# Experts' feed-forward tiles: a two-buffer loop rewritten as straight code with layer 2 a tile behind layer 1

## The reference

```python
hn2 = _layernorm(x, ln2_g, ln2_b).reshape(-1, h)
logits = hn2 @ gate_w + gate_b
idx = jnp.argmax(logits, axis=-1)
mid = jax.nn.relu(jnp.einsum('th,ehf->etf', hn2, w1) + b1[:, None, :])
y = jnp.einsum('etf,efh->eth', mid, w2) + b2[:, None, :]
moe = y[idx, jnp.arange(hn2.shape[0])]
return x + moe.reshape(b, s, h)
```

## Time and profile before

| what | us |
|---|---|
| median of 3 runs | 1405.19 (1399.92 to 1406.61) |
| profiled execution, from first to last instruction (span) | 1443.4 |
| attention stage, to about | 1056 |
| sorting stage, to the first layer 1 | 1094.95 |
| first layer 1 to the last tile's layer 1 | 329.63 |
| last layer 1 to the end of the span | 18.8 |

### The profile page before, as it was taken

How to read it: one execution, slowest core, us unless ns; L and a number is a source line. 1 busy time by engine, 2 the same in 40 slices (tenths; PEclk the granted TensorE clock), 3 DMA queues, 4 the chain that set the end, 5 groups by cost and what they waited for, 6 DMA issues and landing times. The chain is left out here.

```text
span 1443.4 us, 27529 instructions
## 1 busy us (share of the span) xinstructions
PE 1296.1 (90%) x7138; PEld 922.7 (64%) x7138; DVE 942.6 (65%) x6185; ACT 854.2 (59%) x2061; POOL 682.9 (47%) x816
## 2 busy tenths in 40 slices
PE   7868799999999999999999999989828888888886
PEld 6445665666667567576566666655417778877775
DVE  4878979987997996997998899444162222222221
ACT  2335588788697787878878879778611222222221
POOL 3566373553555456346356355320133556655553
PEclk9989999999999999999999999999857999999998
DMA  5210651641842663374274174185132552554451
GB/s 183 86 54 37 155 97 41 166 90 37 180 97 63 129 133 78 85 158 83 73 157 93 35 179 92 42 202 90 44 108 85 179 172 66 195 194 154 154 178 23
DMA packets 104988, 161.15 MB, mean 112 GB/s; under 512 B 35058, under 2 KB 58232, under 8 KB 100760
## 3 DMA queue, kind: packets, MB, share of 16 engines
q1 hardware_dynamic: 86760, 106.51, 31.6%
q0 software_dynamic: 18096, 53.19, 11.6%
HBM read 161.81 MB, written 46.53 MB: 144 GB/s over the span
## 5 line engine op out<-in xcount | busy, mean ns | idle before, releaser
L1013 ACT ACTIVATE pt<-fr 128x512 f32<-128x512 f32 x512 | 277.0, 617 | 25.7 <-PE fr L613 22.5
L1244 DVE CUSTOM_DVE_ANT_0 over<-fr,over 128x256 f32<-128x256 f32 x512 | 198.0, 419 | 85.8 <-ACT over L1023 79.2
L1023 ACT ACTIVATE over<-fr 128x256 f32<-128x256 f32 x512 | 178.7, 391 | 52.9 <-PE fr L613 48.5
L613 PE MATMUL fr<-qs,ks 128*128 128x512 f32 x512 | 189.1, 452 | 3.7 <-DMA qs<-cT 1.3
L613 PE MATMUL fr<-ks,qs 128*128 128x256 f32 x512 | 170.0, 350 | 7.7 <-DVE nmax L1244 3.7
L1358 POOL TENSOR_TENSOR m<-m,e 128x1024 f32<-128x1024 f32 x32 | 75.9, 2370 | 184.9 <-DVE m L1180 184.9
L613 PEld LDWEIGHTS fr<-qs,ks 128*128 128x128 f32 x512 | 87.1, 188 | 86.5 <-issue 50.5
L613 PE MATMUL fr<-kd,qs 128*128 128x256 f32 x512 | 137.0, 282 | 0.0
L814 PE MATMUL ob<-pt,v 128*32 128x512 f32 x1024 | 136.4, 605 | 0.6 <-ACT pt L1013 0.5
L613 PEld LDWEIGHTS fr<-ks,qs 128*128 128x128 f32 x512 | 97.1, 190 | 43.6 <-DVE nmax L1244 25.0
L613 PE MATMUL xs<-VW,pT 128*128 128x256 f32 x512 | 120.0, 389 | 1.8 <-issue 1.7
(11 more groups left out here) (211 smaller groups left out, 2943.7 us busy)
## 6 DMA issues: line engine op xcount, KB each, us to landing
parts_d<-parts SPq DMA_DIRECT2D x32, 512.0 KB, 4.2
ks<-parts_d SPq DMA_DIRECT2D x128, 128.0 KB, 3.9
qs<-parts_d SPq DMA_DIRECT2D x128, 128.0 KB, 4.1
xy_d<-xy SPq DMA_DIRECT2D x32, 256.0 KB, 4.0
kd<-diff_d SPq DMA_DIRECT2D x128, 64.0 KB, 4.0
xyf<-xy_d SPq DMA_DIRECT2D x32, 256.0 KB, 4.2
rows_d<-row SPq DMA_DIRECT2D x32, 256.0 KB, 3.4
diff_d<-diff SPq DMA_DIRECT2D x16, 256.0 KB, 2.3
```

What stands on the lines that cost most here:

```text
L613: return pe.matmul(o, l, r, start=first, stop=last)
L1013: act.activation(pt[:, t % 2, h, :], fr_bank(b, "st", 16 * g + n)[:, :], ACT.Exp, scale=D ** -0.5)\
L1023: act.activation(over[:, (16 * g + n + 64 * b) % NREL, :], fr_bank(b, "fs", 16 * g + n)[:, S // 2:S], ACT.Relu)\
L1244: v.tensor_tensor_reduce(rest, fr_bank(b, "fs", 16 * g + n)[:, 0:S // 2], rest, 1.0, -BIG, ALU.add, ALU.max, nmax[:, g % 2, 4 * h + t:4 * ...
```

## The change

- The loop is gone: all 39 tiles are straight code, and waits compare with constants.
- PE's order becomes: layer 1 of n+1, `turn` of n+2, layer 2 of n. ACT and DVE follow: relu of n+1 comes ahead of the work on tile n's output.
- `rows` and `w1s` have three buffers (`NBUF`), asked for three tiles ahead; `w2s` keeps two and is asked for when layer 2 of n-1 is done, for n+1.
- b2 is repeated for all 128 partitions on the host and joined to the rows of w2 (128 x 2304 floats); the gather of b2 is gone. `resb` of a tile now waits for its w2 rows.
- All gather indices are made once (`wix`, `tix`); the copies to `gix` and `sid` are gone.

```diff
-            def tile(j, q, more, last=False):
-                pe.wait_ge(turned_out[q], reads(j, 1, 1))
-                pe.wait_ge(w1_in[q], reads(j, 16, 16))
...
-                if not last:
-                    turn(j + q, 1 - q)
-                pe.wait_ge(w2_in[q], reads(j, 16, 16))
-                pe.wait_ge(mid_act[q], reads(j, 1, 1))
...
-                    v.tensor_scalar(gix[:, q, :], rec[:, bass.ds(2 * j + q + 2, 1), :].rearrange("p a c -> p (a c)"),
-                                    0.0, None, ALU.add).then_inc(gix_ready[q], 2)
...
+            v.tensor_scalar(wix[:, :, :], wrow[:, :, :], float(P), dc("part"), ALU.mult, ALU.add).then_inc(weights_known, 1)
...
+            v.tensor_scalar(tix[:, :], EO[1][:, 0:ETILES], float(TOK), None, ALU.add).then_inc(tokens_known, 1)
...
+            turn(0)
+            turn(1)
+            first_layer(0)
+            pe.wait_ge(tokens_known, 1)
+            for n in range(ETILES):
+                if n + 1 < ETILES:
+                    first_layer(n + 1)
+                if n + 2 < ETILES:
+                    turn(n + 2)
+                second_layer(n)
...
+            def residual(n):
+                q = n % 2
+                dve.wait_ge(rows_in[n % NBUF], 16 * (n // NBUF + 1))
+                dve.wait_ge(w2_in[q], 16 * (n // 2 + 1))
+                wait(dve, ot_ready[q], n // 2)
+                v.tensor_tensor(resb[:, q, :], rows[:, n % NBUF, DM:2 * DM], w2s[:, q, FT * DM:], ALU.add)\
+                 .then_inc(resb_ready[q], 1)
...
+            middle(0)
+            residual(0)
+            for n in range(ETILES):
+                if n + 1 < ETILES:
+                    middle(n + 1)
+                    residual(n + 1)
+                finish(n)
...
+            fetch_w1(0)
+            fetch_w2(0)
+            fetch_w1(1)
+            fetch_w2(1)
+            fetch_w1(2)
+            pool.wait_ge(tokens_known, 1)
+            for n in range(NBUF):
+                fetch_rows(n)
+            for n in range(ETILES + 1):
+                q = n % 2
+                if n + NBUF < ETILES:
+                    pool.wait_ge(turned[q], n // 2 + 1)
+                    pool.wait_ge(resb_ready[q], n // 2 + 1)
+                    fetch_rows(n + NBUF)
+                    pool.wait_ge(mid_act[q], n // 2 + 1)
+                    pool.wait_ge(mid_dve[q], n // 2 + 1)
+                    fetch_w1(n + NBUF)
+                if 1 <= n < ETILES - 1:
+                    pool.wait_ge(l2_full[1 - q], (n - 1) // 2 + 1)
+                    pool.wait_ge(resb_ready[1 - q], (n - 1) // 2 + 1)
+                    fetch_w2(n + 1)
+                if n > 0:
+                    scatter(n - 1)
```

More of the change, by code:

```diff
@@ L400, in pair @@
             return [sem(f"{name}{n}") for n in range(2)]
-        gix_ready = pair("gix_ready")
-        rows_in, w1_in, w2_in, b2_in = pair("rows_in"), pair("w1_in"), pair("w2_in"), pair("b2_in")
+        weights_known, tokens_known = sem("weights_known"), sem("tokens_known")
+        rows_in, w1_in = [[sem(f"{name}{n}") for n in range(NBUF)] for name in ("rows_in", "w1_in")]
+        w2_in = pair("w2_in")
         turned, turned_out = pair("turned"), pair("turned_out")
@@ L1438, in program @@
         past = sb("past", [P, ETILES, E])
[L1439 to L1445, removed]
+        keep = sb("keep", [P, 2, ETILES])
+        expert = sb("expert", [P, ETILES])
+        wrow = sb("wrow", [P, 2, ETILES])
+        token = sb("token", [P, ETILES])
+        wix = sb("wix", [P, 2, ETILES], U32)
+        tix = sb("tix", [P, ETILES], U32)
+        rows = sb("rows", [P, NBUF, 2 * DM])
         znT2 = sb("znT2", [P, 2, KT, P])
-        w1s = sb("w1s", [P, 2, W1COLS])
-        w2s = sb("w2s", [P, 2, FT, DM])
-        b2s = sb("b2s", [P, 2, DM])
+        w1s = sb("w1s", [P, NBUF, W1COLS])
+        w2s = sb("w2s", [P, 2, W2COLS])
         mid = sb("mid", [P, 2, FT, P])
@@ L1456, in dc @@
             return dcon[:, a:a + n]
[L1458 to L1472, removed]
         block = ctx.enter_context(nc.Block())
@@ L1528, in _ @@
             settle(v.tensor_reduce(ex, past[:, :, :], AX.X, ALU.add))
-            v.memset(keep[:, 0:2], 0.0)
+            v.memset(keep[:, 0, 0:NBUF], 0.0)
+            v.memset(keep[:, 1, 0:2], 0.0)
             settle(v.tensor_scalar(ex, ex, float(E - 1), None, ALU.min))
[L1531 to L1535, removed]
+            v.tensor_tensor(keep[:, 0, NBUF:], expert[:, NBUF:], expert[:, 0:ETILES - NBUF], ALU.is_equal)
+            settle(v.tensor_tensor(keep[:, 1, 2:], expert[:, 2:], expert[:, 0:ETILES - 2], ALU.is_equal))
+            settle(v.scalar_tensor_tensor(wrow[:, :, :], keep[:, :, :], float(E),
+                                          ex.unsqueeze(1).to_broadcast((P, 2, ETILES)), ALU.mult, ALU.add))
+            v.tensor_scalar(wix[:, :, :], wrow[:, :, :], float(P), dc("part"), ALU.mult, ALU.add).then_inc(weights_known, 1)
             settle(v.tensor_tensor(base[:, :], cum[:, c, :], cum[:, 0, :], ALU.subtract))
@@ L1586, in tile, with finish @@
[L1586 to L1590, removed]
-                v.tensor_tensor(ot[:, q, :], EO[q][:, 0:DM], resb[:, q, :], ALU.add).then_inc(ot_ready[q], 1)
-            tiles(dve, tile)
+            def finish(n):
+                q = n % 2
+                dve.wait_ge(l2_full[q], n // 2 + 1)
+                dve.wait_ge(resb_ready[q], n // 2 + 1)
+                wait(dve, scattered[q], 16 * (n // 2))
+                v.tensor_tensor(ot[:, q, :], EO[q][:, 0:DM], resb[:, q, :], ALU.add).then_inc(ot_ready[q], 1)
@@ L1600, in _, with turn, first_layer @@
               .then_inc(count_full, 1)
-            def turn(j, q):
-                pe.wait_ge(rows_in[q], reads(j, 16, 16))
+            def turn(n):
+                q = n % 2
+                pe.wait_ge(rows_in[n % NBUF], 16 * (n // NBUF + 1))
+                wait(pe, turned_out[q], n // 2)
                 for k in range(KT):
-                    ins = pe.transpose(ET[q][:, k * P:(k + 1) * P], rows[:, q, k * P:(k + 1) * P], ident[:, :])
+                    ins = pe.transpose(ET[q][:, k * P:(k + 1) * P], rows[:, n % NBUF, k * P:(k + 1) * P], ident[:, :])
                 ins.then_inc(turned[q], 1)
-            def tile(j, q, more, last=False):
-                pe.wait_ge(turned_out[q], reads(j, 1, 1))
-                pe.wait_ge(w1_in[q], reads(j, 16, 16))
+            def first_layer(n):
+                q = n % 2
+                pe.wait_ge(turned_out[q], n // 2 + 1)
+                pe.wait_ge(w1_in[n % NBUF], 16 * (n // NBUF + 1))
+                wait(pe, mid_act[q], n // 2)
+                wait(pe, mid_dve[q], n // 2)
                 for half in range(2):
@@ L1636, in _, with turned_to @@
             ins.then_inc(tokens_full, 1)
-            turn(0, 0)
-            tiles(pe, lambda j, q, more: tile(j, q, more, isinstance(j, int) and 2 * j + q == ETILES - 1))
+            turn(0)
[8 more added lines that the diff above has]
+                second_layer(n)
         @block.scalar
         def _(act):
-            def turned_to(j, q):
-                act.wait_ge(turned[q], reads(j, 1, 1))
+            def turned_to(n):
+                q = n % 2
+                act.wait_ge(turned[q], n // 2 + 1)
                 for k in range(KT):
@@ L1647, in turned_to, with middle @@
                 ins.then_inc(turned_out[q], 1)
-            def tile(j, q, more):
-                act.wait_ge(l1_full[q], reads(j, 2, 1))
+            def middle(n):
+                q = n % 2
+                act.wait_ge(l1_full[q], 2 * (n // 2) + 1)
+                wait(act, l2_full[q], n // 2)
+                bias = w1s[:, n % NBUF, KT * FF:]
                 for f in range(FT // 2):
-                    ins = act.activation(mid[:, q, f, :], EH[2 * q][:, f * P:(f + 1) * P], ACT.Relu,
-                                         bias=w1s[:, q, KT * FF + f:KT * FF + f + 1])
+                    ins = act.activation(mid[:, q, f, :], EH[2 * q][:, f * P:(f + 1) * P], ACT.Relu, bias=bias[:, f:f + 1])
                 ins.then_inc(mid_act[q], 1)
[L1656 to L1660, removed]
+            turned_to(0)
+            turned_to(1)
+            middle(0)
+            for n in range(ETILES):
+                if n + 1 < ETILES:
+                    middle(n + 1)
+                if n + 2 < ETILES:
+                    turned_to(n + 2)
         @block.gpsimd
@@ L1683, in _, with fetch_rows @@
[L1683 to L1704, removed]
+            def fetch_rows(n):
+                gather(rows[:, n % NBUF, :], rows_d, tix[:, n:n + 1], rows_in[n % NBUF], TOK)
@@ L1705, in tile, with fetch_w1, fetch_w2, scatter @@
+            def fetch_w1(n):
+                gather(w1s[:, n % NBUF, :], w1b, wix[:, 0, n:n + 1], w1_in[n % NBUF], E * P - 1)
+            def fetch_w2(n):
+                gather(w2s[:, n % 2, :], w2b, wix[:, 1, n:n + 1], w2_in[n % 2], E * P - 1)
+            def scatter(n):
+                q = n % 2
+                pool.wait_ge(ot_ready[q], n // 2 + 1)
```

(10 more changed lines are left out.)

42 lines of the change are left out of this document (19 added, 23 removed).

## The result

The changed kernel takes 1464.75 us (median of 4 runs, 1460.54 to 1468.91) against 1405.87 for the kernel before beside it: a ratio of 1.0436 [1.041, 1.0463], 4.4% slower, where 1396 was forecast.

A forecast was written before the change was run, and what follows sets the result against it. PE was taken to bound the kernel, with late-message waits in the experts' stage mostly the profiler's. Stall -11, start +1, changes of expert +1 to 2: about -9 from the 1405 median, 1396 us; range 1355 to 1412.

The forecast's parts named there:

- The late messages: Experts' stage: PE's messages of finished work reach DVE and ACT up to 2.5 us late, mostly in the profiled execution.
- The first case: Experts' stage: waits mostly the profiler's, timed runs lose little; 1388 to 1408, centre 1396, chance 0.50.
- The left-over stall: Experts' stage: part of the 54 us excess still present in timed runs, 6 to 16 us, taken as 11.
- Order of PE: Layer 2 of n after layer 1 of n+1: saves 54 us in the profile, 6 to 16 in timed runs.
- straight code: Experts' tiles without the loop: instruction fetches cost 0 to 1 us in all; bound 1 us for each of some 20.
- Joined b2: b2 in w2's rows: 0.13 MB less in each tile, as much more in each load of w2; worth 0.
- index copies: DVE's 0.16 and 0.15 us a tile removed: worth 0, and 0.07 at the very end.
- The hole: Layer 2 of a tile: PE idle between 1220.4 and 1222.48, waiting for DVE's late relu; predicted to go.
- Start: First tiles: later first weights and rows, and `turn` of tile 1 ahead of layer 1, lose 0.3 to 1.5, taken as 1.
- POOL: POOL's gathers: 0.75 us spare a tile becomes about 2; changed waits are met within a plain tile, cost 0.
- The rival that ended slower: Changes of expert: w2 lands 2.3 us late in 14 loads, +32 us, 1428; range 1410 to 1430, chance 0.12.
- Third buffer: Rows asked for three tiles ahead: worth 0 to 4.6 us; extra w1 loads, 3.8 us of DMA, hidden beside PE.

The follow-up runs named there:

- the second profile: The kernel before, unchanged, profiled once more: 1405.71 us, span 1403.9 us.
- run 7: Changed kernel with w2's gather ahead of rows and w1, but PE, ACT and DVE in the order of the kernel before: 1399.95 us.
- run 8: The kernel before with its hardware loop over tiles written out as straight code: 1403.9 us, ratio 1.0001.
- b2_apart: Changed kernel with b2 gathered by itself again just ahead of w2, `resb` waiting for b2 instead of w2: 1460.2 us.
- no_reload: Changed kernel with all weight gathers after each buffer's first fill out of bounds, so they move nothing: 1393.33 us.
- Runs 1 and 5: Changed kernel with w2's gather ahead of rows and w1: 1393.74 us; changed kernel with four row buffers, rows waiting for `resb` of n-1: 1393.56 us.
- run 9: Changed kernel with a third w2 buffer, w2 asked for n+2 where n+1 was, POOL's order kept: 1388.5 us.
- w2_first: Changed kernel with the gather of w2 for n+1 ahead of the gathers of rows and w1 for n+3: 1393.74 us.
- run 10: Changed kernel with w2's gather ahead of rows and w1, and two w1 buffers instead of three: 1435.17 us.

## Why the prediction was wrong
**The late messages: right.** The first case, that most of the 54 us belong to the one profiled execution, holds: the second profile has no such waits. The left-over stall was given as 6 to 16. It is 285.2 - 275.5, less the 2 of the slow clock, so about 8. The 6 had put some 10 us around the span; they are 1.8 (1405.71 and 1403.9).

**Order of PE, straight code: right. Joined b2, index copies: not shown by themselves.** The hole is gone, and the order is worth 5 to 6 us (run 7), the low end of what was given. Unrolling is worth 0 (run 8); the bound of 1 us a fetch came from no row. `b2_apart` is about as slow as the changed kernel, but both have the circle, so it doesn't price the joining. The copies weren't tried alone.

**Start: taken as 1, is about 0.** From the last matmul of the sorting to the first layer 1 it is 6.6 us in both kernels.

**POOL: the step that failed.** It reads: "The waits ahead of POOL's gathers change: rows of n+3 wait for `resb` of n, and behind them stand w1, w2 and the scatter. In a plain tile all of these are met within the tile: 0." For a plain tile this is so: 6.1 to 6.8 us around, under 7.25. But the sum then had only 1 to 2 us for all changes of expert, and weights are loaded 34 times after the first tiles (20 of w1, 14 of w2, the 37.55 MB by which this queue differs from that of `no_reload`), so that 26 of the 39 tiles had 5 us or more from w2's issue to `resb`. I named the wait and what was queued behind it, but took it for met, without adding up the way back: `resb` of n waits for w2 of n, and so the wait closes on itself. The sum could be made from rows I had: three spacings of POOL of 1.3 and a landing of 8.3 are 12.2, against 7.25 for a tile. It came out at 9.0 to 13.3, and 76.0 us of the stage went where 1 to 2 were put. Runs 1 and 5 open the circle at two different points, run 9 lets it span two tiles, and each takes the whole loss away.

**The rival that ended slower: right in kind, too small and too unlikely.** It had w2 late at changes of expert, 14 loads of 2.3 us, 1428 in all, at 0.12. It counted each load by itself, from an issue point at which POOL was taken to be free, with 11.1 us to land. Its last sentence on this, that `resb` of n+1 holds back POOL's next gathers, is the mechanism, but no price was put on it. In a circle the tiles' losses add up: of w1 as well as of w2 each load lengthens it, and only PE's lead and the plain tiles at 6.1 make up for it. The loss is 349.4 - 273.4 = 76.0 us in the stage. By the PEld rows 55.5 of it is waiting for w2, which leaves 20.5 for PE's work at a lower clock.

**The clock was in no term.** PE waited 4.0 us up to 1132.33 and 5.0 up to 1172.96, and from 1131.3 and 1172.3 on the granted clock was 0.50, 1.2 GHz for 2.4, for 6.8 us each time. After a wait of 1.8 us at 1151.47 it stayed at full. The nine stretches add up to 47.7 us, and PE was busy in 40.9 of them; at full clock this work takes half of that, so 20.5 us are lost, just what the waits leave of the 76.0. The Trainium skill ("TensorE: Matmul & The Clock Gate", section on HAM oscillation) puts the loss at the throttled time multiplied by 1 - 1.2/2.4. By that it would be 23.9; the trace has 20.5, since PE stood idle for 6.8 of the 47.7. The length of a wait alone doesn't tell whether the clock falls: all seven waits of 4.0 us or more have such a stretch at their end, but so have two of 2.3 to 2.4 us (up to 1298.1 and 1349.0), and two of 3.4 to 3.5 (up to 1266.1 and 1361.4) have none.

**Third buffer: right that its bytes are hidden, wrong about its worth.** Extra loads cost nothing (`three_w2` moves the most and is the fastest). But 0 to 4.6 was the worth of asking earlier in the kernel before; with w2 at the head of POOL's list a third w1 buffer is worth 41 us (run 10).

Had the circle not been there, the sum would have held: 1396 against 1393.74 for `w2_first`. That is in part luck: the 11 taken for the stall was some 3 too much, and the 2 to 3 put on for the start and the changes of expert weren't there either, and the two cancel.

## What to carry over
When an engine issues DMAs from one list in order, follow every wait in the list back to the DMA that it depends on: if the same DMA of the next step stands behind the wait, add up the circle (landing, the work behind it, the issues in between) and compare it with the time of one step. Where it is longer, ask one step earlier with one more buffer, or move the issue ahead of the wait; the bytes of an additional reload cost nothing here, up to a mean DMA share of 0.63. And waits of PE cost more than their length: in this kernel 55.5 us of them brought 20.5 us more, since PE went on at half clock after nine of them, for 3.4 to 6.9 us each. Before you compare the same stretch of two orders, count what work lies in it: here one layer 2, 3.4 us, was in one and not in the other.

## What was not expected of the hardware
- One execution of the kernel before had PE's messages up to 2.5 us late in the experts' stage alone, and a span of 1443.4 us; the next had none, and 1403.9. What made it so stays open; none of the other profiles showed it. A second profile would have told it at once.
- A small gather takes longer behind what was asked for before it in its queue: b2, 0.13 MB, took 3.7 to 7.7 us from issue to its first user, 3.7 to 4.0 where no weights moved. A w2 gather whose indices are all out of bounds took 2.2 us at the least, and more behind a real load of w1.
- Weights asked for in time can be gathered again at no cost: 57.54 MB (`w2_first`) and 19.99 MB (`no_reload`) in this queue gave 1393.74 and 1393.33 us.
